# A decoder layer on one core: state-space work of the next sequence moved into the stage before, routing and W2 sums reordered

## The chip, the core and the metric

The kernel runs on one core of a Trainium2 chip. It has five engines with their own instruction queues: TensorE (PE, with weight loads listed as PEld), VectorE (DVE), ScalarE (ACT), GpSimd (POOL) and SyncE (SP, here used for DMA only). Each queue is worked off in order; semaphores make one engine wait for another. The metric is the device time of one execution in microseconds.

## The reference

Four sequences of 256 tokens with 256 channels go through three blocks, each followed by residual and layer norm:

```python
x = _layernorm(x + _L0_attn_ref(x, ...))          # retention, 16 heads, group norm, SiLU gate
x = _layernorm(x + _L0_xattn_ref(ctx_1024, x, ...))  # state-space block on ctx, gated by silu(x)
x = _layernorm(x + _L0_ffn_ref(x, ...))           # 2 of 8 LoRA experts
# state-space block: 256 channels, 16 states, 256 steps
u = silu(causal_conv4(in_proj @ ctx) + conv_b)
dt_lo, Bm, Cm = split(x_proj @ u)
delta = softplus(dt_proj @ dt_lo + dt_proj_b)
state = state * exp(delta * A) + (delta * u) * Bm ;  y = sum_n(state * Cm) + D * u ;  y = y * silu(z)
# experts: for each of the 2 chosen experts k of a token
x1 = x @ W1.T + lora1 ; x3 = x @ W3.T + lora3 ; h = silu(x1) * x3
out += (h @ W2.T + lora2(h)) * rw[k]              # rw: the two top probabilities, normalised
```

## The kernel before

The work is a pipeline over the four sequences. `batches` calls `stage(b, fb)` on every engine: stage 0 does retention and state space of sequence 0 alone; stages 1 to 3, a hardware loop (`Fori`), do retention and state space of sequence `b` together with the experts of `fb = b - 1`; the last stage does the experts of sequence 3.

A stage has a start (`first` or `later`), a loop over 14 slots `n` and a tail. The slots are `MAIN`: chunk `m` of the 896 hidden channels (7 chunks of 128) for the chosen expert `k` (0 or 1). For each slot TensorE runs `base` (W1, W3 on x2, once per chunk: 12 fp32r matmuls of 256 columns) and `hidden` (the LoRA part, 12 more); ScalarE a tanh; VectorE two products (`fs`, then `fq`, here called halves); GpSimd the product with the expert's weight `rwT` (L532) and, for k = 1, the sum `xsums[m]`; TensorE `shrink` (A2) two slots later. In the tail TensorE sums W2 over `xsums` (`down`, 7 times 4 matmuls) and adds B2 in PSUM bank `acc`; VectorE adds the residual (`r3`), normalises and SyncE stores.

The state-space scan is cut into 16 units of 128 x 512. `SCANS` says which slot does which unit. A unit is: ScalarE `decays` (two Exp), GpSimd `drive_unit` (L450, du times a row of B from DRAM), VectorE `scan` (L1246) and `times_c` (L1256), and TensorE `add_states`, four transposing matmuls that add it into `acc`. The ring of units has four places, so a drive waits for the add of the unit four before it. Two units share one pair of rows of B and C that SyncE fetches in `spread`.

Before the scans a stage needs: `context` (input projection, gen bank `IN`), `conv` on VectorE (L1196, six steps of 256 columns), tanh, `u` (L1199), `low_rank` (`DBL`), `step_size` matmuls (`DT`), ScalarE `softplus` (L613 Abs, L617 Exp, L619 Ln, L607 Relu; Ln lies in another activation table than Exp and Tanh), VectorE `step_size` (L1220 to L1228) and GpSimd `du` (L491). All of this stands in `later`, at the start of the stage.

Also in `later`: for the experts of `fb`, the transposes of x2, the router's logits, `route` on VectorE (L1462 to L1489, 24 small dependent steps, 22 of them in part 1), the flip of the routing rows (`rt`), `spread_rows`, the experts' low-rank inputs (`expert_inputs`, A1 and A3, into `a2p`), `masked_inputs` and the split of them into high and low parts `am`. Retention needs Q, K, V, GATE projections, then in slots 0 to 4 eight `scores`, `decayed` and `values`, the group norm in slots 4 to 7, the output projection at n = 9 and `r1` at n = 10 (L1411), its statistics and GpSimd root (L476), the normalised `x1` at n = 12 (L647). At the end comes the gate of the state-space block: tanh of x1 (L775), `zs` (L1417), its transposes `token_z`, `zT` (L641), `r2` (L1423, L1425), `x2` (L647).

PSUM: two `gen` banks used in turn in the order of `LATER` and `GEN_END`; `xf` banks 0 and 1 for hidden slots, bank 2 is `acc`; `a2p` two banks; `ret` for retention; `acc` for y and then for the W2 sums, which is why `down` waits until `r2` has read y:

```python
if b is not None:
    need(pe, "r2_ready", b, 2)
    for m in range(FM - 1):
        down(fb, m)
```

## Time and profile before

| | us |
|---|---|
| median of 3 runs | 509.28 |
| lowest, highest | 505.58, 509.33 |
| the profiled execution | 509.72 |
| its span, first to last instruction | 508.0 |
| TensorE busy | 407.3 (80%) |
| VectorE busy | 360.5 (71%) |
| GpSimd busy | 271.6 (53%) |
| ScalarE busy | 200.8 (40%) |

The profile is of one execution. Busy shares are sums over the span; ends of matmuls are modelled and follow one another closely, so their lengths overlap a little. In a timeline a row gives the start, the length of the group, engine, line, operation, tiles, the number of instructions, and in brackets how long the engine stood idle before it and what ended that. Nearly all matmuls have line 792, a helper, and are told apart by their tiles.

### The profile page before, as it was taken

What the parts mean: (1) busy time and instruction counts of PE and PEld (TensorE: products, weight loads), DVE (VectorE), ACT (ScalarE), POOL (GpSimd) and SP (SyncE); (2) the same over time, 40 slices, a digit from 0 to 9 for tenths busy, and PEclk for the clock granted to TensorE, in tenths of its full rate; (3) what the DMA queues carried; (4) which work ended last, traced back from release to release, by engine and by line L of the source; (5) the groups of instructions that cost most, each with busy time, mean ns of one, the idle gap of its engine ahead of it and who ended that gap; (6) DMA issues with size and microseconds to landing.
All of it is one profiled execution on the core that took longest, in us unless ns stands there. A gap on an engine that the chain in (4) does not pass through costs nothing.

```text
span 508.0 us, 7806 instructions
## 1 busy us (share of the span) xinstructions
PE 407.3 (80%) x2416; PEld 330.7 (65%) x2416; DVE 360.5 (71%) x657; ACT 200.8 (40%) x467; POOL 271.6 (53%) x245
## 2 busy tenths in 40 slices
PE   3748535598799878986999878976999868789994
PEld 2433324376679767864779767764779757679993
DVE  4347999677879997377789996488789994642224
ACT  2757244258543322358443322367442322141100
POOL 6239975334854885207745975208546973033331
PEclk9979656789899989999799989998899999959999
DMA  6592654003021220011111210030112100000000
GB/s 213 95 249 86 201 169 157 22 3 105 11 70 47 83 53 21 20 43 65 41 41 55 70 63 12 22 85 22 41 41 83 48 14 1 21 1 1 1 1 21
DMA packets 16542, 30.44 MB, mean 60 GB/s; under 512 B 2040, under 2 KB 5376, under 8 KB 16384
## 3 DMA queue, kind: packets, MB, share of 16 engines
q1 hardware_dynamic: 16224, 28.27, 18.5%
q10 hardware_dynamic: 288, 1.84, 1.0%
q14 instruction: 20, 0.16, 0.1%
q8 instruction: 10, 0.16, 0.1%
HBM read 28.66 MB, written 1.44 MB: 59 GB/s over the span
## 4 chain that ended last, share of the span: by engine, by line
PE 38%; issue 25%; DVE 23%; POOL 6%; ACT 5%; DMA 1%; DVEq 1%; SPq 0%; POOLq 0%; ACTq 0%
PE xf L792 15%; DVE ring L1246 12%; PE gen L792 9%; PE a2p L792 6%; PE acc L792 4%; PE ret L792 3%; DVE fth L1365 2%; DVE ring L1256 2%; POOL ring L450 1%; POOL rs L476 1%; DMA wattn_sb<-in_wattn 1%; ACT am L654 1%; DVE work L1370 1%; DVE gscale L1402 1%; POOL wsplit L459 1%
## 5 line engine op out<-in xcount | busy, mean ns | idle before, releaser
L450 POOL TENSOR_TENSOR ring<-cv,brow 128x512 f32<-128x512 f32 x64 | 104.4, 1640 | 27.8 <-PE acc L792 18.6
L1246 DVE TENSOR_TENSOR_SCAN ring<-decay,ring 128x512 f32<-128x512 f32 x64 | 102.6, 1603 | 2.1 <-POOL ring L450 2.1
L792 PE MATMUL xf<-am,wsplit 128*128 128x256 f32 x672 | 99.4, 299 | 5.0 <-DVE am L1326 5.0
L792 PEld LDWEIGHTS xf<-am,wsplit 128*128 128x128 f32 x672 | 89.4, 199 | 11.7 <-DVE am L1326 8.1
L532 POOL TENSOR_TENSOR work<-work,rwT 128x256 f32<-128x256 f32 x56 | 55.9, 998 | 64.8 <-DVE work L1370 64.8
L568 ACT ACTIVATE decay<-dt_w,nega 128x255 f32<-128x255 f32 x128 | 57.6, 498 | 72.9 <-DVE ring L1246 72.8
L792 PE MATMUL a2p<-work,wff_sb 128*128 128x256 f32 x288 | 75.2, 390 | 0.5 <-POOL work L532 0.5
L792 PE MATMUL acc<-ident,ring 128*128 128x128 f32 x256 | 43.6, 299 | 39.5 <-DVE ring L1256 39.2
L1256 DVE TENSOR_TENSOR ring<-ring,crow 128x512 f32<-128x512 f32 x64 | 68.3, 1067 | 3.2
L792 PEld LDWEIGHTS acc<-ident,ring 128*128 128x128 f32 x256 | 32.3, 152 | 54.4 <-DVE ring L1256 49.7
L748 ACT ACTIVATE fth<-xf 128x256 f32<-128x256 f32 x56 | 21.0, 375 | 97.2 <-PE xf L792 97.1
L792 PEld LDWEIGHTS a2p<-work,wff_sb 128*128 128x128 f32 x288 | 51.7, 193 | 10.5 <-issue 4.5
L792 PE MATMUL xf<-x2s,wsplit 128*128 128x256 f32 x336 | 53.3, 313 | 0.7 <-ACT rwT L728 0.7
L1365 DVE SCALAR_TENSOR_TENSOR fth<-fth,xf 128x256 f32<-128x256 f32 x56 | 23.2, 414 | 37.1 <-ACT fth L748 37.1
L792 PEld LDWEIGHTS xf<-x2s,wsplit 128*128 128x128 f32 x336 | 47.0, 208 | 2.9 <-ACT rwT L728 1.0
L476 POOL TENSOR_TENSOR rs<-ve,mhalf 128x2 f32<-128x2 f32 x12 | 11.8, 986 | 56.1 <-DVE ve L1284 56.1
L665 ACT ACTIVATE qm<-q_sb,headblk 128x128 f32<-128x128 f32 x96 | 30.4, 391 | 20.4 <-PE gen L792 20.4
L792 PE MATMUL gen<-qm,kT 128*128 128x512 f32 x64 | 35.9, 646 | 2.3 <-POOL qm L482 2.3
L1263 DVE TENSOR_TENSOR sc<-gen,dmask 128x512 f32<-128x512 f32 x32 | 22.0, 686 | 20.0 <-PE gen L792 19.5
L491 POOL TENSOR_TENSOR cv<-dt_w,u 128x512 f32<-128x512 f32 x4 | 5.1, 1264 | 55.0 <-DVE dt_w L1228 55.0
L792 PE MATMUL gen<-xT_sb,wattn_sb 128*128 128x256 f32 x96 | 27.5, 437 | 4.9 <-DMA wattn_sb<-in_wattn 3.1
L792 PEld LDWEIGHTS gen<-xT_sb,wattn_sb 128*128 128x128 f32 x96 | 20.6, 220 | 9.9 <-DMA wattn_sb<-in_wattn 3.8
(175 smaller groups left out, 582.7 us busy)
## 6 DMA issues: line engine op xcount, KB each, us to landing
brow<-bc_dram SPq DMA_DIRECT2D x32, 256.0 KB, 3.5
crow<-bc_dram SPq DMA_DIRECT2D x32, 256.0 KB, 3.3
work<-in_wsp SPq DMA_DIRECT2D x2, 896.0 KB, 7.6
work<-in_wsp ACTq DMA_DIRECT2D x2, 896.0 KB, 5.4
wff_sb<-in_wff SPq DMA_DIRECT2D x2, 896.0 KB, 6.4
wattn_sb<-in_wattn SPq DMA_DIRECT2D x1, 1280.0 KB, 5.9
xT_sb<-in_xT SPq DMA_DIRECT2D x4, 256.0 KB, 3.5
xn_sb<-in_x SPq DMA_DIRECT2D x4, 256.0 KB, 2.5
```

Of the source, the lines that this page charges most:

```text
L450: pool.tensor_tensor(ring[:, i % RING], du[:, j].unsqueeze(1).broadcast_to([P, UN, S]), brow[:, c % 2], ALU.mult).then_inc(sem["drive_read ...
L476: pool.tensor_tensor(dst[:], src[:], mhalf[:], ALU.pow).then_inc(sem[done], 1)
L491: pool.tensor_tensor(du[:], delta[:], u[:], ALU.mult).then_inc(sem["du_ready"], 1)
L532: pool.tensor_tensor(xs[:, n % 4], fq[:, n % 2], rwT[:, k], ALU.mult).then_inc(sem["xs_ready"], 1)
L568: act.activation(decay[:, i % 2, n, 1:], delta[:, j, 1:], ACT.Exp, scale=nega[:, j, s_:s_ + 1]).then_inc(sem["decay_ready"], 1)
L665: last = act.activation(qm[:, i % 2, h], q_sb[:, t, chunk * P:(chunk + 1) * P], ACT.Copy, scale=headblk[:, row:row + 1])
L748: act.activation(fth[:, n % 2], xf[XF_BANK[X_MAIN + n]][:, 0], ACT.Tanh, scale=0.5).then_inc(sem["th_ready"], 1)
L792: return pe.matmul(o, l, r, skip_group_check=True, **kw)
L1246: dve.tensor_tensor_scan(unit, flat(decay[:, i % 2]), unit, 0.0, ALU.mult, ALU.add).then_inc(sem["state_ready"], 1)
L1256: dve.tensor_tensor(unit, unit, crow[:, c % 2], ALU.mult).then_inc(sem["out_ready"], 1)
L1263: dve.tensor_tensor(sc[:, i % 2], gen[(G_SC + i) % 2][:].rearrange("p (h i) -> p h i", h=4), dmask[:, h0:h0 + 4], ALU.mult).then_inc(sem[" ...
L1365: dve.scalar_tensor_tensor(fs[:, n % 2], fth[:, n % 2], 1.0, o[:, 0], ALU.add, ALU.mult).then_inc(sem["s_ready"], 1)
```

## The change

- The loop over the stages is written out: no `Fori`, every wait is on a constant. The order of the gen banks is one list over all stages.
- For the next sequence `b + 1` these move from the start of its stage into stage `b`: `context` (n = 8), convolution (9), `u` and `DBL` (10), `DT` (11), softplus and step sizes (12), `du` and the first drives (12, 13), decays 0 and 1 (13); then, in the tail, scans 0 and 1 (`EARLY`), Q, decays 2 and 3, drives 2 and 3. Scans 2 to 4 (`PROLOGUE`) run in the start of the stage, 5 to 15 in slots 0 to 9.
- The transposes of x2, the logits and the routing of sequence `b` run in the tail of stage `b`, ahead of B2 on TensorE, instead of at the start of the next stage.
- The W2 sums and B2 accumulate in `ret` instead of `acc`; `down` 0 to 4 run right after the last shrink, 5 and 6 after the logits. `xf` bank 2 is `ret`.
- The expert weights: expert 0 has weight 1 and expert 1 the ratio of the two; the common factor `share` is multiplied in `r3`. So the product with k = 0 goes from VectorE straight into `xs`, without GpSimd. Routing has two steps fewer (22, 20 of them in part 1).
- `r1`, `dt_e`, `cth`, `dt_abs` live in other buffers (`qm`, `gth`). SyncE stores `b - 2` and reloads inputs between the B and C rows.

The diff, cut to its core:

```diff
 
-SCANS = [[0], [1], [2], [3, 4], [5], [6], [7], [8, 9], [10], [11, 12], [13, 14], [15], [], []]
+FIRST_SCANS = [[0], [1], [2], [3, 4], [5, 6], [7, 8], [9, 10], [11, 12], [13], [14], [15], [], [], []]
+SCANS = [[5], [6], [7], [8], [9], [10], [11, 12], [13], [14], [15], [], [], [], []]
+EARLY, PROLOGUE = [0, 1], [2, 3, 4]
+N_IN, N_CONV, N_U, N_DBL, N_DT, N_STEP = 8, 9, 10, 10, 11, 12
+
+
+def scans(b, n):
+    return (SCANS if b else FIRST_SCANS)[n] if b is not None else []
+
+
 PARTS = ((0, 0), (0, 1), (1, 0))
 POOL_MASKED = (2, 3)
 AM_ORDER = [0, 2, 1, 3]
 LAG = 2
...
 
             stage(0, None)
-            with eng.Fori(1, B) as b:
+            for b in range(1, B):
                 stage(b, b - 1)
             stage(None, B - 1)
...
                 for c in range(DS // UN):
+                    if c == 2 and b >= 2:
+                        store(b - 2)
+                    if c == 3 and b + 1 < B:
+                        reload(b + 1)
 
...
                     need(pool, "y_part", b, i - RING + 2)
+                elif b > 0:
+                    need(pool, "y_part", b, i - RING + 1)
...
+                    step_input(b)
                     drive_unit(b, 0)
                     drive_unit(b, 1)
-                    if fb is not None:
-                        for i in POOL_MASKED:
-                            masked(b, i)
+                elif b is not None:
+                    drive_unit(b, 4)
+                    drive_unit(b, 5)
+                    for i in POOL_MASKED:
+                        masked(b, i)
+                    cross_queries(b)
+                    drive_unit(b, 6)
                 if fb is not None:
 
...
                                                ).then_inc(sem["xsum_ready"], 1)
+                    if b is not None and n == 12 and b + 1 < B:
+                        step_input(b + 1)
+                        drive_unit(b + 1, 0)
                     if b is not None and n == 13:
                         root(b, ve, rs, "r2_ready", 9, "r2_pow")
+                        if b + 1 < B:
+                            drive_unit(b + 1, 1)
                         if fb is None:
                             split_low(range(3 * PER_W, BLOCKS))
+                if b is not None and b + 1 < B:
+                    drive_unit(b + 1, 2)
+                    drive_unit(b + 1, 3)
+                    residual(b + 1)
...
                 for j in range(2):
                     act.activation(dt_abs[:, j], g[:, j], ACT.Abs, bias=v_("dtb")[:, j:j + 1]).then_inc(sem["dt_parts"], 1)
-                if isinstance(b, int):
+                if b == 0:
                     positive(b, g)
                 need(act, "dt_parts", b, 2)
                 act.activation(dt_e, dt_abs[:], ACT.Exp, scale=-1.0).then_inc(sem["dt_exp"], 1)
                 need(act, "dt_exp", b, 1)
...
+            def tail(b):
+
+                need(act, "keep_ready", b, 0)
+                normed(b, r2, x2, "r2_shift", "x2_ready")
+                need(act, "xf_filled", b, X_X2 + 1)
+                need(act, "xs_ready", b, 0)
+                act.wait_ge(sem["w_low_b3"], PER_W)
+                act.activation(x2T, xf[XF_BANK[X_X2]][:], ACT.Copy).then_inc(sem["x2T_ready"], 1)
+                act.activation(x2s[:, 0], xf[XF_BANK[X_X2]][:], ACT.Copy).then_inc(sem["x2T_ready"], 1)
+                if b + 1 < B:
+                    queries(b + 1)
+                    start_y(b + 1)
+                need(act, "rt_step", b, 2)
+                act.activation(le[:], lg[:], ACT.Exp).then_inc(sem["lg_exp"], 1)
+                if b + 1 < B:
+                    for i in EARLY:
+                        decays(b + 1, i + 2)
+
             def later(b, fb):
...
-                    low_rank(b)
-                    softplus(b)
                     masked(b, 1)
...
-                    decays(b, 0)
+                    decays(b, PROLOGUE[0] + 2)
                 am_high(fb, (2, 3))
                 if b is not None:
-                    decays(b, 1)
+                    for i in PROLOGUE[1:]:
+                        decays(b, i + 2)
...
                             if i + 2 < UNITS:
                                 decays(b, i + 2)
+                        if b + 1 < B:
+                            if n == N_IN:
+                                conv_input(b + 1)
+                            if n == N_CONV:
+                                conv_tanh(b + 1)
+                            if n == N_DBL + 1:
+                                low_rank(b + 1)
+                            if n == N_STEP:
+                                softplus(b + 1)
                         if n == 7:
                             need(act, "gn_step", b, 12)
...
-                    need(act, "keep_ready", b, 0)
-                    normed(b, r2, x2, "r2_shift", "x2_ready")
+                    tail(b)
 
             batches(act, stage)
...
+
                 if b is not None:
-                    token_values(b)
-                    low_rank(b)
...
                 need(pe, "a2_ready", fb, 0)
                 expert_inputs(0, A1)
                 if b is not None:
-                    step_size(b)
+                    token_values(b)
                 expert_inputs(1, A3)
                 if b is not None:
+                    token_keys(b)
                     project(b, "GATE", wg)
+                    start_y(b)
+                    for i in EARLY:
+                        add_states(b, i)
                 base(fb, 0)
 
                 xf_free(fb, X_RT)
...
                     scores(b, 1)
+                    for i in PROLOGUE[:2]:
+                        add_states(b, i)
                 else:
                     base(fb, 1)
...
-                                start_y(b, fb)
-                            else:
-                                for i in SCANS[n - 1]:
-                                    add_states(b, i)
+                            for i in (scans(b, n - 1) if n > 0 else PROLOGUE[2:]):
+                                add_states(b, i)
                         if 1 <= n <= 4:
...
+                        if n == N_IN and b + 1 < B:
+                            context(b + 1)
+                        if n == N_DBL and b + 1 < B:
+                            low_rank(b + 1)
+                        if n == N_DT and b + 1 < B:
+                            step_size(b + 1)
...
                                 for k in range(2):
                                     last = mm(g[:, t], ro[:, k, t * P:(t + 1) * P], wo[:, k], start=(k == 0), stop=(k == 1))
                             last.then_inc(sem["gen_filled"], 1)
                 if fb is not None:
+                    shrink(fb, len(MAIN) - 1)
                     if b is not None:
-                        need(pe, "r2_ready", b, 2)
-                        for m in range(FM - 1):
+                        need(pe, "ro_lin", b, 2)
+                        for m in range(W2_FIRST):
                             down(fb, m)
-                    shrink(fb, len(MAIN) - 1)
-                    down(fb, FM - 1)
+                if b is not None:
+                    flip_x2(b)
+                    if b + 1 < B:
+                        need(pe, "x_in", b + 1, 16)
+                        project(b + 1, "Q", wq)
+                    logits(b)
+                if fb is not None:
+                    for m in range(W2_FIRST if b is not None else FM - 1, FM):
+                        down(fb, m)
                     need(pe, "a2_ready", fb, 3)
                     for t in range(NT):
                         for k in range(2):
-                            last = mm(acc[:, t], a2m[:, 0, k, t * P:(t + 1) * P], B2[:, k], start=False, stop=(k == 1))
...
-                    conv(b)
                     token_values(b)
-                need(dve, "x2T_ready", fb, 2)
-                dve.tensor_tensor(x2s[:, 1], xf[XF_BANK[X_X2]][:], x2s[:, 0], ALU.subtract).then_inc(sem["xl_ready"], 1)
-                route(fb, 0)
-                if b is not None:
                     token_keys(b)
-                route(fb, 1)
-                if b is not None:
-                    step_size(b)
+                    scan(b, PROLOGUE[0])
+                    times_c(b, PROLOGUE[0])
                     chunk_state(b)
                 need(dve, "a_filled", fb, 2)
...
                     gate_silu(b)
+                    for i in PROLOGUE[1:]:
+                        scan(b, i)
+                        times_c(b, i)
 
...
+                            need(dve, "xs_used", fb, max(n - 3, 0))
+                            need(dve, "xsum_ready", fb, MAIN[n - 4][0] + 1 if n >= 4 else 0)
+                            product = xs[:, n % 4]
+                        else:
+                            need(dve, "xs_ready", fb, max(m - 1, 0))
+                            product = fq[:, m % 2]
+                        dve.tensor_tensor(product, fs[:, n % 2], o[:, 1], ALU.mult).then_inc(sem["q3_ready"], 1)
+                    if b is not None and n == 11:
                         norm_shift(b, mv, rs, nm, "r1_pow", "r1_shift")
...
                             norm_stats(b, r1, st, mv, ve, "r1_ready", 1)
+                        if n == N_CONV and b + 1 < B:
+                            conv(b + 1)
+                        if n == N_U and b + 1 < B:
+                            gated_conv(b + 1)
...
                             dve.scalar_tensor_tensor(zs[:], zth[:], 1.0, x1[:], ALU.add, ALU.mult).then_inc(sem["r2_ready"], 1)
+                            if b + 1 < B:
+                                step_size(b + 1)
                             if fb is None:
...
+                early = EARLY if b is not None and b + 1 < B else []
+                for i in early[:1]:
+                    scan(b + 1, i)
+                if b is not None:
+                    norm_shift(b, mv, rs, nm, "r2_pow", "r2_shift")
+                for i in early[:1]:
+                    times_c(b + 1, i)
                 if fb is not None:
                     second_input(fb, 1)
                     need(dve, "a2_ready", fb, 2)
                     dve.tensor_tensor(a2m[:, 0], a2m[:, 0], a2m[:, 1], ALU.add).then_inc(sem["a2_ready"], 1)
                 if b is not None:
-                    norm_shift(b, mv, rs, nm, "r2_pow", "r2_shift")
+                    need(dve, "x2T_ready", b, 2)
+                    dve.tensor_tensor(x2s[:, 1], xf[XF_BANK[X_X2]][:], x2s[:, 0], ALU.subtract).then_inc(sem["xl_ready"], 1)
+                for i in early[1:]:
+                    scan(b + 1, i)
+                if b is not None:
+                    route(b, 0)
+                for i in early[1:]:
+                    times_c(b + 1, i)
+                if b is not None:
+                    route(b, 1)
                 if fb is not None:
                     need(dve, "down_done", fb, 1)
                     need(dve, "keep_ready", fb, 1)
-                    dve.tensor_tensor(r3[:], acc[:], keep[:], ALU.add).then_inc(sem["r3_ready"], 1)
-                    norm_stats(fb, r3, st3, mv3, ve3, "r3_ready", 1)
+                    for t in range(NT):
+                        dve.scalar_tensor_tensor(r3[:, t], ret[:, t], share[:, fb % 2, t:t + 1], keep[:, t], ALU.mult, ALU.add
+                                                 ).then_inc(sem["r3_ready"], 1)
+                    norm_stats(fb, r3, st3, mv3, ve3, "r3_ready", 2)
                     norm_apply(fb, r3, mv3, rs3, yo, "r3_pow", "y_ready")
 
```

## Rows read from the trace of the kernel before

**Rows 1.** Stretches table: stretch and length in us, busy time by engine (instructions), PEclk, DMA, GB/s
```profile
0.00:95.80 95.80, 50.33 (x223) 32.00 (x223) 67.50 (x97) 45.74 (x103) 58.96 (x65) 0.79 0.54 158
95.80:123.60 27.80, 25.80 (x108) 18.85 (x108) 19.11 (x55) 15.95 (x37) 11.65 (x11) 0.87 0.13 41
...
235.80:306.20 70.40, 62.07 (x425) 52.84 (x426) 62.75 (x86) 27.69 (x69) 49.25 (x37) 0.93 0.17 53
306.20:322.80 16.60, 14.29 (x73) 11.81 (x72) 7.84 (x20) 4.06 (x8) 5.20 (x6) 1.00 0.01 1
322.80:348.00 25.20, 21.61 (x109) 16.25 (x107) 16.76 (x56) 15.73 (x36) 7.96 (x8) 1.00 0.20 57
...
435.20:452.20 17.00, 12.37 (x64) 10.40 (x63) 10.90 (x41) 4.73 (x10) 0.69 (x1) 0.77 0.04 16
452.20:508.00 55.80, 48.70 (x321) 45.07 (x320) 16.59 (x41) 6.78 (x17) 19.87 (x25) 0.96 0.02 6
```

**Rows 2.** Instructions on tile `ring`, one stage (213.6 to 325.8): ns min/median/max
```profile
L1246 DVE TENSOR_TENSOR_SCAN ring<-decay,ring x16: 1211/1514/2286, 238.9 to 304.4; 128x512 f32<-128x512 f32 x16
...
L1256 DVE TENSOR_TENSOR ring<-ring,crow x16: 680/968/1595, 241.7 to 306.4; 128x512 f32<-128x512 f32 x16
```

**Rows 3.** Timeline of TensorE, products 8 and 12 of stage 2: start, length
```profile
280.27 1.57 PE L792 MATMUL xf<-am,wsplit 128*128 128x256 f32 x12
...
304.58 1.56 PE L792 MATMUL xf<-am,wsplit 128*128 128x256 f32 x12
```

**Rows 4.** Timeline of stage 2's end, VectorE, the last row TensorE
```profile
308.32 0.70 DVE L1417 SCALAR_TENSOR_TENSOR kT<-kT,q_sb 128x512 f32<-128x512 f32 x1 [0.47 <-ACT kT L775]
...
313.01 0.88 DVE L1425 TENSOR_TENSOR dt_w<-dt_w,q_sb 128x512 f32<-128x512 f32 x1
...
314.93 3.62 PE L792 MATMUL acc<-wff_sb,sc 128*128 128x256 f32 x16
```

**Rows 5.** Timeline at the loop's seam, VectorE, then TensorE, stage 2
```profile
216.60 2.46 DVE L1196 SCALAR_TENSOR_TENSOR cv<-xpad,cwh,cv 128x256 f32<-128x256 f32 x6 [2.35 <-issue]
...
220.59 1.05 PE L792 MATMUL gen<-u,wssm_sb 128*40 128x256 f32 x4 [2.50 <-DVE u L1199]
```

**Rows 6.** Timeline around the first product, TensorE, the last row VectorE
```profile
229.79 0.61 PE L792 MATMUL acc<-ident,rt 128*20 128x128 f32 x4
...
241.01 1.12 PE L792 MATMUL acc<-ident,yT 128*128 128x128 f32 x4 [2.79 <-ACT yT L636]
...
238.91 2.29 DVE L1246 TENSOR_TENSOR_SCAN ring<-decay,ring 128x512 f32<-128x512 f32 x1
```

**Rows 7.** Timeline of ScalarE: softplus of stage 2, normalisation ahead of z
```profile
224.83 0.84 ACT L613 ACTIVATE yT<-gen,vec_sb 128x256 f32<-128x256 f32 x2 [1.91 <-PE gen L792]
...
226.35 1.28 ACT L619 ACT_TABLE_LOAD   x1
227.64 0.63 ACT L619 ACTIVATE yT<-ring 128x512 f32<-128x512 f32 x1
...
306.54 1.08 ACT L647 ACTIVATE q_sb<-dt_w,nm,rs 128x256 f32<-128x256 f32 x2
```

**Rows 8.** Groups by line, GpSimd, the same stage
```profile
L450 POOL TENSOR_TENSOR ring<-cv,brow 128x512 f32<-128x512 f32 x16 | 25.8, 1622 | 6.4 <-PE acc L792 6.2 <-POOL cv L491 0.2
L532 POOL TENSOR_TENSOR work<-work,rwT 128x256 f32<-128x256 f32 x14 | 15.2, 1085 | 13.2 <-DVE work L1370 13.2
```

**Rows 9.** Timeline of stage 2's start, VectorE, the last row GpSimd
```profile
219.76 0.69 DVE L1199 SCALAR_TENSOR_TENSOR u<-ring,cv 128x512 f32<-128x512 f32 x1 [0.69 <-ACT ring L586]
...
222.81 0.16 DVE L1469 TENSOR_REDUCE t<-le 128x2 f32<-128x16 f32 x1
...
227.47 0.43 DVE L1220 TENSOR_SCALAR dt_w<-ring 128x512 f32<-128x512 f32 x1
...
230.25 1.26 POOL L491 TENSOR_TENSOR cv<-dt_w,u 128x512 f32<-128x512 f32 x1 [14.03 <-DVE dt_w L1228]
```

**Rows 10.** Timeline of VectorE, end of stage 0
```profile
95.71 0.69 DVE L1423 TENSOR_TENSOR dt_w<-acc,yT 128x512 f32<-128x512 f32 x1 [0.90 <-ACT yT L641]
```

308 lines of the change are left out of this document (152 added, 156 removed).

## The prediction

> **What bounds the kernel now.** I read the stretches table first. One loop stage takes 112.2 us and I cut it at three marks. H is the first expert product (`hidden(fb, 0)`), X the end of `hidden(fb, 12)`, T the end of the B2 product. H to X takes 70.4, X to T 16.6, T to the next H 25.2. The whole span is then 123.6 to the first H, twice 112.2, 104.2 for stage 3 (348.0 to 452.2), and 55.8 for the last: 508.0 [rows 1]. In none of them is one engine at full load, so each has its own last wait.
>
> In H to X the last part is VectorE's. It carries the 16 scan units of the stage, each a scan of 1.51 and a product with C of 0.97 in the median [rows 2]. From the start of product 8 to that of product 12 TensorE takes 24.3 us [rows 3]. Its own work there (four products, two bases, four shrinks, eight to nine adds, one output projection) comes to about 17 at 0.23 us for an fp32 matmul of 256 columns (3.62 for 16, [rows 4]) and 1.4 to 1.5 for twelve fp32r ones. So 7 us are waits for VectorE.
>
> From T to H the chain runs through the seam of the loop: VectorE starts the convolution after 2.35 us that are put down to issue, works 2.5 on it, and TensorE waits 2.5 for `u` [rows 5]. The routing flip comes at 229.79 [rows 6] and H 6.0 later. From X to T the chain is normalise, tanh, `zs`, transpose, `zT`, `r2`, and then TensorE's W2 sums [rows 4, 7].
>
> **The change part by part.** Nothing large disappears. Seven of 14 GpSimd products per stage (1.09 each, [rows 8]) and two routing instructions go; the rest moves to another place. What counts is therefore which waits open and close.
>
> *T to H.* Context, Q, flip, logits, DBL and DT leave this stretch. TensorE has left K, A1, V, A3 and GATE (40 matmuls, 9.0), key transpose and `y` start (1.0), the adds of units 0 and 1 (0.9) and base 0 (1.5): 12.4, then from the routing flip to H the 6.0 of before, since the ScalarE/VectorE chain between them stays. That is 18.4 against 25.2, a gain of 6.8. The routing does not hold it up: 22 instructions of part 1 take 4.66 (222.81 to 227.47, [rows 9]), the new one has 20, and I find it ending 2 us after T, while its reader comes 12 us after T.
>
> At H something new is last. TensorE now has `add_states(3)` before `hidden(fb, 0)`, and it needs `times_c(3)`. VectorE does unit 3 only after `gate_silu`: the scan would begin where that of unit 0 begins now, 238.91, and takes 2.29 there [rows 6], its product 0.7 to 1.0 [rows 2]. So H's matmuls start 6 us later than the mark. Before, TensorE stood until 241.01 in any case, for `yT` [rows 6]; the net loss is 2 (bounds 0 and 6), and I book it in H to X.
>
> *H to X, stages 1 and 2.* VectorE does 13 units instead of 16 after H, gains the convolution (2.46) and `u` (0.69) [rows 5, 9]. That is 7.4 less, 3.2 more. It lets TensorE run product 8 to 12 at its own pace: 17.5 with the three moved small projections, plus a new wait. `low_rank(b+1)` stands in TensorE's queue at n=10 behind nothing else, and its `u` comes on VectorE after product 10's two halves, `r1`, its statistics: 2.9 us idle. 20.7 against 24.3, a gain of 3.6. With the 2 from above H to X becomes 68.8.
>
> *X to T, stages 1 and 2.* ScalarE at n=12 now runs tanh 12, then `softplus(b+1)`, and only then the normalisation and tanh of the z chain. Softplus is Abs, Exp, a table load, Ln, Relu: 224.83 to 228.27 plus 0.8 for the two Relu, 4.2. The tanh then needs its table back, 1.28 more [rows 7]. The z tanh ends 7.6 after X, `zs` 8.3 (now it starts at 308.32, 2.1 after X, [rows 4]), and TensorE, which is through at X+4.2, waits 4. VectorE goes on with `step_size`, 2.7 (227.47 until GpSimd starts at 230.25, [rows 9]), then halves 13 and `r2`: ready at X+13.0 against 7.7 now [rows 4]. GpSimd's last xs product sits behind `step_input` and `drive_unit(b+1, 0)` (1.26, [rows 9], and 1.62, [rows 8]) that wait for the same step size, so the shrink 13 comes at X+14.9. From there TensorE has shrink, seven W2 sums, flip, Q, logits, B2: 4+28+8+8 matmuls at 0.23 plus 1.3, 12.1. T = X+27.0; the price is 10.4, bounds 7 (chains overlap better) and 14. I add 0.5 for VectorE's token values, which now follow `r3`.
>
> The period is 68.8 + 27.0 + 18.9 = 114.7, 2.5 more than 112.2; low 109, high 119.
>
> *Stage 0.* It gets all moved work and gives none up: convolution 2.5 and unit 15 now ahead of `r1` (1.9 at the shortest times of [rows 2]), then the serial chain `u`, DBL, `dbl`, DT, softplus, table load (0.7+1.1+0.4+1.1+4.2+1.3 = 8.8), `step_size` between `zs` and `r2` (1.7 net), scan 0 of the next sequence ahead of the shift (1.2). Now `r2` starts at 95.71 [rows 10]; I expect 110. The first H moves from 123.6 to 139.7: +16. Bounds: +8, if most of the chain lies beside other work, and +19.
>
> *Stage 3.* No next sequence: no softplus in the tail. H to X loses 2.7 of projections and the 2.9 wait, 63.2. X to T: flip and logits inside, the gaps filled, 17.3. T to H: A1, A3, base 0, then 7.2 as now from the routing flip, 12.5 against 17.0. 93.0 against 104.2, a gain of 11.2 (bounds 9 and 15). The last stage stays 55.8.
>
> *Sum.* 139.7 + 2 x 114.7 + 93.0 + 55.8 = 517.9. The profiled execution lies 1.7 above its span (509.72 against 508.0), so 519.6; it is 0.4 above the median of 509.28. I say 519.
>
> *Loads and buffers.* The new SyncE order puts `store(b-2)` ahead of the B rows for unit 4 and `reload` ahead of those for unit 6. I price them at nothing: the store waits for `y_ready` at about T+6, and unit 4's drive is needed only near H, some 12 us later. If that cover went, its drive (1.62, [rows 8]) and the load ahead of it would come on top of H, bounded by the 6 us that H stands anyway.
>
> **Two rules against the rows.** Softplus has its table load at 226.35, 1.28 long, and the next activation starts at 227.64 [rows 7]. The Trainium skill, page "ScalarE: Activation LUTs", section "What ACT_TABLE_LOAD costs", puts a switch at 2.66 us, with a drain of 1.38 behind the load. The trace shows no such gap; by the page two switches in three tails would make the sum 8 us larger, 528.
> The loop's seam shows 2.35 of issue on VectorE [rows 5]. The Trainium skill, "Runtime: NRT & Kernel Launch", section "Instruction fetch mechanics", says that a taken branch can break the sequential prefetch and prefers unrolled code. The row agrees; but as VectorE is not last from T to H any more, it is inside the 6.8. If it came on top, the sum would be 515.
>
> **The rivals.**
> *Faster, the two engines stop hindering each other.* A unit costs VectorE 2.48, but the shortest scan took 1.21 and the shortest product 0.68 [rows 2]: 0.59 a unit, 38 us over 64 units. GpSimd sheds 7 x 1.09 a stage. If 22 of the 38 came back where VectorE is last (stage 0 and H to X), H to X would come to the 62 us that TensorE is busy [rows 1] and stage 0 would pay 8 instead of 16: 519 - 2 x 6.8 - 8 = 497. It decides from 15 us on (below 504), some 40% of the 38. For it: VectorE is last in stage 0. Against: `drive_unit` (16 x 1.62, [rows 8]) stays as it is, and work squeezed into less time overlaps more. 0.25.
> *No change, the costs of stage 0 are half hidden.* +8, and a period of 112 as before: 131.6 + 224 + 93 + 55.8 + 1.7 = 506; with +12, 510. Here the softplus chain would lie beside VectorE's last scans. 0.20.
> *Slower still, TensorE's clock.* TensorE stands 4 and then 6 us in the new tail and 6 at H. In 435.2 to 452.2, where it has such waits, the granted clock averages 0.77 of 2.4 GHz, in the three parts of the loop stage 0.93 to 1.00 [rows 1]. If 12 us of tail ran at 1.2 GHz for a half, and H as well, 5 to 6 a stage: 534. 0.13.
> *Forecast*, the moved chain in front of z costs what the seam gives and stage 0 pays once: 513 to 527. 0.42.
>
> **How the numbers follow.** About 1% is what a measurement of this kernel can tell from no change: 504 to 514.4. Slower: 0.42 + 0.13 less a little, 0.54; same 0.20; faster 0.26. The likeliest gives 519, its own range 513 to 527. For 8 in 10 the range must take in part of the faster rival and of the slow one: 498 to 532.
>
> **What would show it.** In the changed profile: ScalarE's Ln load between tanh 12 and the z normalisation; TensorE idle before `token_z` (about 4) and before shrink 13 (about 6); a wait on `times_c(3)` ahead of the first product; the first product at 140 and not near 124; T to H at 18 to 19; stage 3 at 93. Wrong it would be if scan units fell to 2.0 us, if the period were below 110, or if `u` and the step sizes came early enough that `r2` stands no later than 8 after X.

## The result: slower by 5.6%

The changed kernel took 536.67 us (median of 4 runs, 536.15 to 538.09), the kernel before 509.17 beside it; the ratio is 1.0562, 95% interval [1.0511, 1.0613]. The forecast was 519 with a range of 498 to 532. The direction was right; the size was 18 us too small, and the time lies outside the range.

The profiled execution of the changed kernel has a span of 535.3 (before: 508.0). Cut at the same marks H, X and T as before, its stretches table reads as follows (columns as in [rows 1]). H is here only a mark: the routing flip plus 6.0 us (139.49 plus 6.0 for the first), where the first product would start if nothing new stood ahead of it. In the last stage it is the product's own start.

```profile
0.00:145.50 145.50, 77.22 (x345) 51.90 (x345) 97.32 (x156) 68.34 (x154) 77.94 (x78) 0.77 0.41 120
145.50:220.20 74.70, 62.79 (x424) 52.88 (x425) 59.73 (x89) 24.34 (x62) 35.80 (x30) 0.91 0.14 42
220.20:249.20 29.00, 19.02 (x90) 16.18 (x89) 17.38 (x38) 15.46 (x31) 11.94 (x9) 0.82 0.07 23
249.20:266.90 17.70, 16.93 (x92) 13.50 (x91) 10.69 (x34) 7.69 (x20) 5.36 (x5) 1.00 0.35 81
266.90:340.90 74.00, 62.07 (x425) 52.00 (x426) 59.28 (x89) 24.34 (x62) 35.85 (x30) 0.93 0.14 41
340.90:369.30 28.40, 18.88 (x91) 16.04 (x89) 17.41 (x38) 15.46 (x31) 11.95 (x9) 0.82 0.09 28
369.30:387.00 17.70, 16.90 (x92) 13.49 (x90) 10.69 (x34) 7.71 (x21) 5.40 (x5) 1.00 0.18 59
387.00:452.30 65.30, 56.86 (x412) 49.01 (x413) 56.32 (x82) 22.05 (x57) 35.55 (x30) 0.95 0.11 37
452.30:468.90 16.60, 14.98 (x83) 13.08 (x82) 10.27 (x33) 5.37 (x11) 2.15 (x3) 1.00 0.00 0
468.90:478.50 9.60, 8.15 (x50) 6.90 (x49) 6.27 (x22) 3.05 (x6) 0.69 (x1) 1.00 0.08 29
478.50:535.30 56.80, 47.95 (x322) 44.10 (x320) 18.14 (x44) 7.01 (x17) 14.73 (x18) 0.98 0.02 5
```

| part | before | forecast | measured | forecast missed by |
|---|---|---|---|---|
| start to the first H mark | 123.6 | 139.7 | 145.5 | +5.8 |
| stage 1: H to X, X to T, T to H | 70.4, 16.6, 25.2 | 68.8, 27.0, 18.9 | 74.7, 29.0, 17.7 | +6.7 |
| stage 2 | the same | the same | 74.0, 28.4, 17.7 | +5.4 |
| stage 3 | 104.2 | 93.0 | 91.5 | -1.5 |
| last stage | 55.8 | 55.8 | 56.8 | +1.0 |
| span | 508.0 | 517.9 | 535.3 | +17.4 |

Two stretches of the stage stand out. X to T holds 19 us of TensorE work in 29 us, at a granted clock of 0.82; before, it held 14.3 in 16.6 at 1.00 [rows 1]. And H to X, which was to become shorter, is 4 us longer with the same 62 us of TensorE work. TensorE's timeline (start, length, what it did, idle time before it and what ended it) shows where it stands. The row at 152.57 is ahead of the first product, the one at 211.15 ahead of product 11 of stage 1, those from 228.64 on are the tail.

```profile
152.57 1.12 PE L856 MATMUL acc<-ident,ring 128*128 128x128 f32 x4 [7.85 <-DVE ring L1336]
153.33 2.91 PE L856 MATMUL xf<-am,wsplit 128*128 128x256 f32 x12
...
211.15 1.03 PE L856 MATMUL gen<-u,wssm_sb 128*40 128x256 f32 x4 [3.74 <-DVE u L1279]
212.11 2.48 PE L856 MATMUL xf<-am,wsplit 128*128 128x256 f32 x12
...
228.64 0.63 PE L1071 MATMUL gen<-ident,kT 128*128 128x128 f32 x4 [4.27 <-DVE kT L1503]
234.98 2.07 PE L856 MATMUL a2p<-work,wff_sb 128*128 128x256 f32 x4 [5.71 <-POOL work L574]
236.84 3.44 PE L856 MATMUL ret<-wff_sb,xsum 128*128 128x256 f32 x8
```

These are the four waits that the forecast named: unit 3's product, `u`, `token_z`, the last shrink product. It had them at 6, 2.9, about 4 and about 6 us. Behind the first, the second and the last, the same instructions take longer than elsewhere: twelve matmuls of a product 2.91 and 2.48 us instead of the 1.57 of [rows 3], eight W2 matmuls 3.44 instead of 1.9. That is not new at H. The kernel before has it there too, behind its own wait for `yT` (2.79, [rows 6]):

```profile
241.78 2.91 PE L792 MATMUL xf<-x2s,wsplit 128*128 128x256 f32 x12
244.48 2.49 PE L792 MATMUL xf<-am,wsplit 128*128 128x256 f32 x12
```

From H to product 8 TensorE is busy 41.2 of 44.5 us before and 41.4 of 49.6 (stage 1) and 40.7 of 48.9 (stage 2) in the changed kernel, at granted clocks of 0.92, 0.90 and 0.93. So what this part lost is waiting, about 4.9 us a stage, and not slower matmuls.

The chain that leads to the third and fourth wait, on ScalarE, VectorE and GpSimd:

```profile
222.20 1.28 ACT L669 ACT_TABLE_LOAD   x1
223.35 1.02 PE L856 MATMUL a2p<-work,wff_sb 128*128 128x256 f32 x4
223.49 0.63 ACT L669 ACTIVATE gth<-qm 128x512 f32<-128x512 f32 x1
224.03 0.82 ACT L655 ACTIVATE ring<-gen,vec_sb 128x256 f32<-128x256 f32 x2
224.74 1.08 ACT L698 ACTIVATE q_sb<-qm,nm,rs 128x256 f32<-128x256 f32 x2
225.84 1.28 ACT L837 ACT_TABLE_LOAD   x1
227.14 0.63 ACT L837 ACTIVATE kT<-q_sb 128x512 f32<-128x512 f32 x1
...
227.80 0.69 DVE L1503 SCALAR_TENSOR_TENSOR kT<-kT,q_sb 128x512 f32<-128x512 f32 x1 [6.10 <-ACT kT L837]
...
231.08 1.27 POOL L523 TENSOR_TENSOR cv<-dt_w,u 128x512 f32<-128x512 f32 x1 [13.56 <-DVE dt_w L1308]
...
231.71 0.68 DVE L1511 TENSOR_TENSOR qm<-acc,yT 128x512 f32<-128x512 f32 x1
...
234.20 0.72 POOL L574 TENSOR_TENSOR work<-work,ratioT 128x256 f32<-128x256 f32 x1
```

Softplus with its table load stands ahead of z on ScalarE, so `zs` comes 7.6 after X (2.1 before, [rows 4]); the step size stands ahead of `r2` on VectorE; `step_input` and drive 0 stand ahead of the last ratio product on GpSimd. One order was not tried: softplus ahead of tanh 12. The `DT` bank is full at 217.3, and ScalarE stands idle for 5.13 us until tanh 12 starts at 220.41.

### The profile page after: what moved, and what is told of

It reads as the page before. It is cut to its first block and busy times, and to the rows that moved or that the text cites. A ratio compares the mean times of both kernels' runs of the same rounds, so it can differ in the third digit from the quotient of the medians.

```text
span 535.3 us, 6819 instructions
## 1 busy us (share of the span) xinstructions
PE 401.8 (75%) x2412; PEld 329.1 (61%) x2412; DVE 363.5 (68%) x653; ACT 200.8 (38%) x467; POOL 237.4 (44%) x215
## 3 DMA queue, kind: packets, MB, share of 16 engines
q1 hardware_dynamic: 16224, 28.27, 18.1%
## 5 line engine op out<-in xcount | busy, mean ns | idle before, releaser
L478 POOL TENSOR_TENSOR ring<-cv,brow 128x512 f32<-128x512 f32 x64 | 97.7, 1534 | 69.1 <-PE acc L856 44.4
L1326 DVE TENSOR_TENSOR_SCAN ring<-decay,ring 128x512 f32<-128x512 f32 x64 | 101.4, 1585 | 2.1 <-POOL ring L478 2.1
L856 PE MATMUL acc<-ident,ring 128*128 128x128 f32 x256 | 45.6, 310 | 51.7 <-DVE ring L1336 51.7
L856 PEld LDWEIGHTS acc<-ident,ring 128*128 128x128 f32 x256 | 33.9, 157 | 65.8 <-DVE ring L1336 59.7
L1336 DVE TENSOR_TENSOR ring<-ring,crow 128x512 f32<-128x512 f32 x64 | 66.5, 1040 | 3.0
L574 POOL TENSOR_TENSOR work<-work,ratioT 128x256 f32<-128x256 f32 x28 | 23.1, 825 | 94.8 <-DVE work L1454 92.2
L856 PE MATMUL xf<-x2s,wsplit 128*128 128x256 f32 x336 | 49.1, 295 | 0.5 <-ACT ratioT L782 0.5
L856 PEld LDWEIGHTS xf<-x2s,wsplit 128*128 128x128 f32 x336 | 43.0, 191 | 3.2 <-issue 1.4
L856 PE MATMUL gen<-xT_sb,wattn_sb 128*128 128x256 f32 x96 | 25.9, 418 | 6.0 <-DVE vpad L1287 3.1
L1343 DVE TENSOR_TENSOR sc<-gen,dmask 128x512 f32<-128x512 f32 x32 | 21.9, 684 | 9.4 <-PE gen L856 9.1
L856 PEld LDWEIGHTS gen<-xT_sb,wattn_sb 128*128 128x128 f32 x96 | 19.3, 210 | 10.1 <-DMA wattn_sb<-in_wattn 3.6
```

What stands on the lines that cost most here:

```text
L478: pool.tensor_tensor(ring[:, i % RING], du[:, j].unsqueeze(1).broadcast_to([P, UN, S]), brow[:, c % 2], ALU.mult).then_inc(sem["drive_read ...
L574: pool.tensor_tensor(xs[:, n % 4], fq[:, m % 2], ratioT[:], ALU.mult).then_inc(sem["xs_ready"], 1)
L856: return pe.matmul(o, l, r, skip_group_check=True, **kw)
L1326: dve.tensor_tensor_scan(unit, flat(decay[:, i % 2]), unit, 0.0, ALU.mult, ALU.add).then_inc(sem["state_ready"], 1)
L1336: dve.tensor_tensor(unit, unit, crow[:, c % 2], ALU.mult).then_inc(sem["out_ready"], 1)
L1343: dve.tensor_tensor(sc[:, i % 2], g[:].rearrange("p (h i) -> p h i", h=4), dmask[:, h0:h0 + 4], ALU.mult).then_inc(sem["sc_ready"], 1)
```

## The experiments

All numbers are in us. The kernels down to scans_behind start from the changed kernel, those from before_unrolled on from the kernel before; each ratio is to runs of the kernel before on the same chip, so ratios compare better than medians. "First flip" is the start of the first routing flip; a stage is the distance to the next one (stages 1, 2 and 3), "rest" what follows the last flip; these columns are of one profiled execution each. unrolled_relief leaves out expert 0's weight and so computes something else; it shows time only.

| kernel | time | ratio to before, 95% interval | first flip | stages 1, 2, 3 | rest |
|---|---|---|---|---|---|
| before | 509.17 | 1 | 118.3 | 111.5, 112.3, 102.9 | 63.1 |
| changed | 536.67 | 1.0562 [1.0511, 1.0613] | 139.5 | 121.4, 120.1, 92.8 | 61.5 |
| z_first | 531.0 | 1.0432 [1.0387, 1.0476] | 135.4 | 118.5, 119.0, 93.7 | 61.5 |
| dbl_later | 529.72 | 1.0394 [1.0358, 1.043] | 140.4 | 118.0, 116.7, 92.8 | 61.4 |
| add3_later | 543.0 | 1.0649 [1.0608, 1.069] | 139.0 | 122.6, 122.8, 95.5 | 61.5 |
| all_three | 526.04 | 1.0321 [1.0283, 1.036] | 136.1 | 115.1, 116.9, 95.2 | 61.4 |
| unit3_early | 530.86 | 1.0429 [1.0384, 1.0474] | 140.2 | 118.6, 119.0, 90.5 | 61.4 |
| filled_waits | 559.74 | 1.1018 [1.0975, 1.106] | 138.4 | 124.1, 124.8, 108.1 | 61.5 |
| sized_work | 533.09 | 1.0483 [1.044, 1.0527] | 137.6 | 118.3, 118.5, 93.4 | 61.5 |
| reordered | 509.41 | 0.9993 [0.9975, 1.0012] | 136.0 | 109.3, 108.4, 92.1 | 61.5 |
| order_two | 509.61 | 0.9997 [0.9972, 1.0022] | 137.1 | 109.3, 109.2, 91.6 | 61.5 |
| scans_behind | 508.27 | 0.9972 [0.9956, 0.9988] | 136.3 | 106.9, 108.9, 93.1 | 61.4 |
| before_unrolled | 505.77 | 0.9924 [0.9892, 0.9957] | 117.5 | 111.6, 110.5, 100.4 | 62.1 |
| unrolled_relief | 498.84 | 0.9799 [0.977, 0.9829] | 118.7 | 109.0, 108.7, 98.6 | 62.2 |
| only_ratio | 500.21 | 0.9755 [0.9704, 0.9805] | 118.0 | 109.5, 109.3, 100.4 | 61.9 |
| ratio_w2 | 494.07 | 0.9705 [0.9663, 0.9747] | 118.2 | 106.8, 106.5, 98.7 | 61.4 |
| not_moved | 512.57 | 1.0037 [1.0007, 1.0067] | 126.4 | 112.6, 112.6, 96.2 | 61.4 |
| flip_early | 511.36 | 1.0021 [0.9981, 1.0061] | 123.3 | 109.7, 112.6, 102.1 | 62.2 |

### z_first: softplus and step size behind the z chain

```diff
 # ScalarE
-                            if n == N_STEP:
-                                softplus(b + 1)
 ...
                             z_columns(b)
-                                decays(b + 1, 0)
-                                decays(b + 1, 1)
+                                softplus(b + 1)
 # VectorE: step_size(b + 1) and scan 0 behind norm_shift, second_input(fb, 1) and the a2 sum
 # ScalarE: decays 0, 1 behind normed(x2);  GpSimd: step_input, drive 0 behind root(r2)
```

> The changed kernel, with one thing moved: ScalarE's softplus of the next sequence stands behind z_columns instead of ahead of the z normalisation, and what hangs on it (step sizes on VectorE, step_input and drives 0 and 1 on GpSimd, decays 0 and 1) stands behind r2 and its statistics. Theory A (the serial chain softplus, table load, z is what makes the tails long; X to T is 29.0 and 28.4 in stages 1 and 2, and stage 0 ends 22 us later than before): X to T falls to about 19, the first product comes some 9 us earlier than 145.5, three tails give 27 to 30 together: about 508. Theory B (the tail is long because VectorE and GpSimd simply have more to do there, the same work in whatever order): the work stays in the tail, X to T stays at 26 or more, total above 528.

It took 531.0: the time of theory B, but not its mechanism. X to T fell as theory A has it, in stage 1 from 29.0 to 21.3, and x2's flip comes 12 us sooner in stage 0 (108.97 instead of 121.12). Yet the routing flip of stage 0 comes only 4.1 sooner, and T to the next routing flip grew from 11.7 to 17.1 in stage 1. The saved time is taken back there, where TensorE now waits for the value bank that VectorE has to read, and runs the next eight matmuls in 2.96 instead of 1.89:

```profile
247.49 2.96 PE L855 MATMUL gen<-xT_sb,wattn_sb 128*128 128x256 f32 x8 [3.47 <-DVE vpad L1286]
```

VectorE had scan 0 and its product (2.21 and 1.50, beside GpSimd's drives), scan 1, the routing and the last norm ahead of `vpad`. So the order in the tail was a cause, but what it gave was for the most part spent at the next place where TensorE waits for VectorE.

### dbl_later: the u matmuls one slot later

```diff
-N_IN, N_CONV, N_U, N_DBL, N_DT, N_STEP = 8, 9, 10, 10, 11, 12
+N_IN, N_CONV, N_U, N_DBL, N_DT, N_STEP = 8, 9, 10, 11, 12, 12
```

> The changed kernel, with DBL and DT on TensorE one slot later (n = 11 and 12). Theory A (TensorE's 3.74 us ahead of DBL wait for u in vain, and the slower clock behind it costs another 2 to 3): both go, 5 to 6 us in stages 1 and 2; the softplus that is ahead of z starts about 2 later, so 3 to 4 of them stay as gain: about 530. In stage 0, where u comes right after the adds, a loss of 1 to 2. Theory B (the chain to z is last in any case): no gain, 536 to 541.

529.72, as theory A has it: 1.7% of the kernel before for one number. The wait for `u` went from 3.74 to 1.45, and the twelve matmuls of the next product behind it take 1.57 instead of 2.48.

### add3_later: unit 3's add behind the first product

```diff
-                    for i in PROLOGUE[:2]:
+                    for i in PROLOGUE[:1]:
                         add_states(b, i)
 ...
-                            for i in (scans(b, n - 1) if n > 0 else PROLOGUE[2:]):
+                            for i in (scans(b, n - 1) if n > 0 else PROLOGUE[1:]):
```

> The changed kernel, with add_states(3) on TensorE moved from ahead of the first product to behind it. Theory A (TensorE's 7.85 us in front of it are a wait in the wrong place of the queue): the first product starts 6 to 7 us earlier, hidden 2 ends 3 to 5 earlier, at full clock; over stages 1 to 3 that is 9 to 14 us: 523 to 528. Theory B (VectorE sets the pace there, since units 3, 4 and 5 stand ahead of the first halves, whatever TensorE does): TensorE waits at the next bank instead, total within 3 us of 536.7.

543.0, slower by 6 and so outside both theories. The first product did run early, and TensorE then stood at the same result:

```profile
144.41 0.97 PE L856 MATMUL xf<-am,wsplit 128*128 128x256 f32 x6 [0.23 <-DVE am L1401]
145.86 0.97 PE L856 MATMUL xf<-am,wsplit 128*128 128x256 f32 x6 [0.49 <-DVE am L1401]
152.05 1.11 PE L856 MATMUL acc<-ident,ring 128*128 128x128 f32 x4 [5.21 <-DVE ring L1336]
155.86 1.12 PE L856 MATMUL acc<-ident,ring 128*128 128x128 f32 x4 [2.70 <-DVE ring L1336]
156.63 2.91 PE L856 MATMUL xf<-x2s,wsplit 128*128 128x256 f32 x12
159.34 2.57 PE L856 MATMUL xf<-am,wsplit 128*128 128x256 f32 x12
```

5.21 + 2.70 is about the old 7.85. Moving the waiter does nothing when the thing waited for does not come sooner. The stages are 1.2, 2.7 and 2.7 longer. Part of that is in the rows: the base matmuls and product 1 take 2.91 and 2.57 here, in the changed kernel 2.08 and 1.58, and product 1 ends 1.8 us later behind the routing flip. For the rest I have no row.

### all_three: the three edits together

> All three moves together. If each wait is a place in a queue and they add up: 536.7 - 28 - 12 - 8 = 489, faster than the kernel before by 4%. If they hide one another (one wait removed is taken over by the next): 500 to 510. If the moved work itself is what costs, above 515.

526.04, 10.6 below the changed kernel and 17 above the one before; that is 2.4% of before, while the first two alone gave 1.3 and 1.7 (and the third cost 0.9). So the three edits nearly add up (2.1 against 2.4), and the kernel still stands above the 515 that the expectation gave to the moved work itself. The named waits are real, and they are not the whole.

### unit3_early: scan 3 into VectorE's gap

VectorE stands idle for 4.18 at 137, until the KV bank is there. Scan 3 and its product have all their inputs by then.

```diff
-                    scan(b, PROLOGUE[0])
-                    times_c(b, PROLOGUE[0])
+                    for i in PROLOGUE[:2]:
+                        scan(b, i)
+                        times_c(b, i)
                     chunk_state(b)
```

> The changed kernel with scan 3 and its product moved ahead of chunk_state on VectorE, into the 4.18 us in which VectorE stands idle there waiting for the KV bank; scans 4 onward stay. Theory A (order): the 7.85 us that TensorE waits for the product of unit 3 ahead of the first expert product is an accident of VectorE's order, so the wait goes under 1 us, the first product comes 6 us sooner behind the routing flip in stages 1 to 3, the clock dip after it vanishes too, and the kernel takes about 519 us. Theory B (the wait only moves): masked inputs, low parts and scan 4 are as late as before, so TensorE waits at hidden(0) or at unit 4 instead, a stage keeps its length within 1 us and the kernel takes 534 us or more.

530.86, between the two theories: the wait of 7.85 is gone, a wait of 5.21 for unit 4 stands behind the first product in its place, and 2.8, 1.1 and 2.3 a stage are left over as gain. Scan 3 takes 1.22 in the gap, where GpSimd is idle, and took 2.28 at its old place. Where the waited-for work was moved (here) it helped, where the waiter was moved (add3_later) it did not.

### reordered: all of it, and VectorE's tail

z_first, dbl_later and unit3_early, and beyond them:

```diff
 # VectorE's tail: low part of x2, routing, then scans 0 and 1
-                for i in early[:1]:
-                    scan(b + 1, i)
-                    times_c(b + 1, i)
 ...
                 if b is not None:
                     route(b, 0)
+                for i in early[:1]:
+                    scan(b + 1, i)
 ...
 # the last norm of the sequence before behind the next token values and keys
                     token_values(b)
                     token_keys(b)
+                finish(fb - 1)
```

> The changed kernel with softplus behind z_columns (as in z_first), N_DBL, N_DT = 11, 12 (as in dbl_later), scan 3 ahead of chunk_state, and VectorE's tail in the order low part of x2, route, scan 0, scan 1; the residual norm of the sequence before goes behind the next token values and keys, so that GATE's bank comes free earlier. Theory A: the waits add up and each of them stands on the path, so from 526.0 us (three of the edits together) it falls by a further 6 us at scan 3 and 3 us in the tail for each of three stages, to about 500 us, under the kernel before. Theory B: the path has other work right behind each wait (VectorE's whole load of a stage, the clock), and the kernel stays at 515 us or more.

509.41: as fast as the kernel before, 27.3 below the changed one, with the same instructions (TensorE 402.0 us busy, VectorE 362.9, ScalarE 199.9; in the changed kernel 401.8, 363.5 and 200.8). So the loss of the changed kernel against the one before can be undone by order alone. It came out between the 500 of theory A and the 515 of theory B.

### order_two and scans_behind: further in the same direction

```diff
 # order_two
+ TensorE: unit 4 added behind hidden(1)
+ ScalarE: decays 0, 1 behind the two copies of the turned x2; decay 3 behind the keys
 # scans_behind, on top of it
+ VectorE: scans 4 and 5 behind score masks 0, 1 and the first expert product
```

> The kernel of the run reordered with three waits more taken out: TensorE adds unit 4 behind hidden(1) instead of behind hidden(0) (wait of 4.8 to 5.2 us three times), ScalarE makes decays 0 and 1 behind the two copies of the turned x2 instead of ahead of them (TensorE's logits wait 2.1 us), and decay 3 behind the keys (TensorE's keys product waits 7.6 us for kT in the first turn). Theory A: what is left of the change's loss is such waits, so about 4 us a stage and 6 in the first come off 509.4 us: 492 to 497 us, faster than the kernel before. Theory B: VectorE's or TensorE's own work bounds the stage by now (TensorE stands still only where it has nothing that could run): 505 us or more.

> The kernel of the run order_two, with scans 4 and 5 behind the first two score masks and the first expert product on VectorE (and decay 6 behind the first tanh on ScalarE). In order_two VectorE is busy 9.90 of 10 us ahead of the first score mask, with scan 4, its product and scan 5 at 2.3, 1.5 and 2.3 us beside GpSimd's drives, and TensorE waits 5.0 us for that mask, while the first expert product, ready at 254.7, is taken up at 263.4. Theory A (order within VectorE's list): the masks come 6 us sooner, the wait of 4 to 5 us goes, and three stages give 4 us each: about 497 us. Theory B (VectorE's load): scans 4 and 5 are only late elsewhere, the ring is free later and TensorE waits for sums instead: 506 to 512 us.

509.61 and 508.27, both theory B. In order_two the waits that were taken out come back under another name, in the table of TensorE's waits (total, times, longest):

```profile
PE gen L855 <- DVE vpad L1288: 15.2, 4, 7.4
PE ret L855 <- DVE sc L1344: 15.2, 3, 5.2
```

Between 252 and 262 VectorE is busy for 9.90 of 10 us there and TensorE for 4.83. In scans_behind the wait for `sc` is gone, and the waits for scan results are back at 42.2 in all (order_two: 25.2). In these two steps order gave nothing more; that VectorE's load around H is the limit is what the rows suggest, and no run takes load off VectorE in this kernel to show it.

### filled_waits and sized_work: is it the clock?

Idle products into the free retention bank keep TensorE at work in the tail's two waits; the waits and their causes stay.

```diff
+            def idle_work(b, count):
+                need(pe, "ro_lin", b, 2)
+                for k in range(count):
+                    mm(ret[:, k % 2], ident[:], wq[:, k % 2], start=(k == 0), stop=(k == count - 1))
 # filled_waits: 16 ahead of token_z, 22 ahead of the last shrink; sized_work: 9 and 12, stages 1 and 2 only
```

> The changed kernel with idle work on TensorE in its two waits at the end of stages 1 to 3: 16 products of 128x128 by 128x256 float32 into the free retention bank ahead of token_z, and 22 ahead of the last shrink product (W2's first sum clears the bank again). Waits and their causes stay, only TensorE is not idle in them. Theory A (clock): the slower granted clock behind the waits is a loss of its own: shrink 13 takes 1.0 instead of 2.07 us and the first 8 W2 sums 1.9 instead of 3.44, 2.5 us a stage come off in stages 1 and 2, some in 3: 529 to 532 us. Theory B: the waits alone carry the loss: 535 to 539 us.

> As filled_waits, but sized to the waits: 9 idle products ahead of token_z and 12 ahead of the last shrink product, in stages 1 and 2 only (a product took 0.22 us there, so 2 us in a wait of 4.3 and 2.6 in one of 5.7; in filled_waits 16 and 22 of them overran the waits, above all in stage 3, whose waits are short). Theory A (clock): shrink 13 takes 1.0 instead of 2.07 and the first 8 W2 sums 1.9 instead of 3.44 us, so 2.6 us a stage come off: about 531 us. Theory B: nothing: 535 us or more.

filled_waits told little about the time: 22 idle products took 9.66 us in a wait of 5.7, and in stage 3, which has no such waits, they came on top (stage 3: 108.1 instead of 92.8). But its rows behind the waits were at once short. sized_work took 533.09, between its two theories: 0.8% of the kernel before, or 4 us, less than the changed kernel, and the intervals of the two ratios just overlap. So the size rests on the rows. An idle product shows as two matmuls; nine took 4.05 us and twelve 5.35, nearly the whole of the waits and not half, as the expectation has it:

```profile
225.92 0.63 PE L1071 MATMUL gen<-ident,kT 128*128 128x128 f32 x4 [0.39 <-DVE kT L1513]
226.39 5.35 PE L856 MATMUL ret<-wattn_sb,ident 128*128 128x256 f32 x24
232.26 1.13 PE L856 MATMUL a2p<-work,wff_sb 128*128 128x256 f32 x4 [0.53 <-POOL work L574]
233.23 1.89 PE L856 MATMUL ret<-wff_sb,xsum 128*128 128x256 f32 x8
```

The last shrink takes 1.13 instead of 2.07 and the W2 matmuls 1.89 instead of 3.44; the shrink still starts where it did, 14.8 behind X. The granted clock from `token_z` to x2's flip reads 1.00, in the changed kernel 0.64, and X to T is 26.6 instead of 29.0 in stage 1. So the granted clock behind the tail's waits is a loss of its own of about 2 us a stage. The larger part of the 12 us that X to T grew is waits: TensorE is idle 10.0 us in it, before 2.3. What is left is moved work.

### before_unrolled: the loops alone

```diff
-            with eng.Fori(1, B) as b:
+            for b in range(1, B):
                 stage(b, b - 1)
```

> The kernel before with its two loops (all engines' loop over sequences 1 to 3, SyncE's over 1 and 2) written out by Python, nothing else. Theory A: the seam between iterations (2.35 and 2.50 us of issue on VectorE and TensorE ahead of the first conv step and the u matmuls) stands on the path, so 2 or 3 seams give 4 to 7 us: 502 to 505 us. Theory B: it is hidden or comes back as instruction loading: 508 to 510 us.

505.77, 0.8% faster, close to theory A. (The 2.50 that the expectation calls issue on TensorE is its wait for `u` in [rows 5].) VectorE starts the convolution with no gap (before: 2.35 put down to issue, [rows 5]):

```profile
214.44 3.94 DVE L1196 SCALAR_TENSOR_TENSOR cv<-xpad,cwh,cv 128x256 f32<-128x256 f32 x6
```

### unrolled_relief and only_ratio: GpSimd's products

unrolled_relief leaves out expert 0's weight; only_ratio makes the same saving and keeps the result, as the changed kernel does, by the ratio and a common share.

```diff
-                        pool.tensor_tensor(xs[:, n % 4], fq[:, n % 2], rwT[:, k], ALU.mult).then_inc(sem["xs_ready"], 1)
+                        if k == 1:
+                            pool.tensor_tensor(xs[:, n % 4], fq[:, m % 2], rwT[:, k], ALU.mult).then_inc(sem["xs_ready"], 1)
 # only_ratio: ratioT for rwT[:, k]; route with 22 steps; r3 = acc * share + keep
```

> The unrolled kernel before, with the product of expert 0 left out on GpSimd (VectorE writes its masked product straight into xs, so the weight of the first expert is left out of the result; 7 of 14 GpSimd products of 128x256 a stage fall away). Theory A: TensorE's expert products bound this stretch and GpSimd's relief is worth nothing: within 1.5 us of the unrolled kernel. Theory B: fewer GpSimd products let VectorE's scans and products run nearer to 1.21 and 0.69 us, and the shrink products wait less: 4 us or more below the unrolled kernel.

> The unrolled kernel before with the ratio's way of routing of the changed kernel (expert 1 weighted by its ratio to expert 0, the common share applied in the last residual; route with 22 steps instead of 24 and NR 18 instead of 20): the whole of what is asked of GpSimd's relief in unrolled_relief, but with nothing left out. Theory A (GpSimd's 7 products a stage hinder): as fast as unrolled_relief, 498 to 500 us, 9 to 11 us under the kernel before. Theory B (unrolled_relief gained from something else, such as the early store into xs without the weight's wait): 503 us or more.

498.84 and 500.21: some 6 us below before_unrolled, theory B of the first and theory A of the second. From product 8 to 12 of stage 2, where TensorE waits only for scan results, these waits fell from 5.4 to 3.6 us and the stretch from 24.5 to 22.8. The scans:

```profile
L1246 DVE TENSOR_TENSOR_SCAN ring<-decay,ring x64: 1194/1508/2292, 25.4 to 411.9; 128x512 f32<-128x512 f32 x64
```

```profile
L1249 DVE TENSOR_TENSOR_SCAN ring<-decay,ring x64: 1208/1272/2340, 25.3 to 407.0; 128x512 f32<-128x512 f32 x64
```

(the first row is of before_unrolled, the second of unrolled_relief; ns min/median/max). The median overstates it: it jumps from the slow scans to the fast ones. The mean of a scan fell only from 1611 to 1558 ns, 3.4 us over all 64, and VectorE's whole busy time from 364.7 to 359.3.

The mechanism of the rival in which the two engines stop hindering each other is there, and this saving is worth 1.3% on its own. How much of the 1.3% comes of it is open: expert 0's products also reach TensorE without the step on GpSimd, and no run parts the two, since only_ratio does both as well.

### ratio_w2: the W2 sums in retention's bank

```diff
-        xf.append(acc)
+        xf.append(ret)
-                    mm(acc[:, t], xsums[m][:, t * P:(t + 1) * P], W2[:, m], start=(m == 0 and t == 0), stop=False)
+                    mm(ret[:, t], xsums[m][:, t * P:(t + 1) * P], W2[:, m], start=(m == 0 and t == 0), stop=False)
-                        need(pe, "r2_ready", b, 2)
+                        need(pe, "ro_lin", b, 2)
```

> The kernel of the run only_ratio with the W2 and B2 sums in retention's bank (they no longer wait for r2, and the routing flip and mask differences use that bank too), while x2's flip and the routing stay in the head of the next stage. Theory A (the bank is not what makes not_moved 12 us slower than only_ratio, the early routing ahead of the next convolution on VectorE is): as only_ratio or up to 4 us below it, since the wait of 1.5 us a stage for r2 goes: 496 to 501 us. Theory B (the bank costs): 504 us or more.

494.07, ratio 0.9705: the fastest kernel of the study, faster than both. The medians are 6 us below only_ratio; the two ratios, 0.9755 and 0.9705, have intervals that overlap, so how much this step gives is not settled. In the rows, TensorE no longer waits for `r2` ahead of the sums (1.48 a stage in only_ratio), and a stage fell from 109.4 to 106.7.

### not_moved and flip_early: x2's flip ahead of the last sums

```diff
 # not_moved, on ratio_w2: TensorE's order at the end of a stage
+                    for m in range(5):
+                        down(fb, m)
+                if b is not None:
+                    flip_x2(b)
+                    logits(b)
+                    for m in range(5 if b is not None else FM - 1, FM):
+                        down(fb, m)
 # and: ScalarE's copies and exponential, VectorE's low part and routing in the tail
 # flip_early: the exponential, the low part and the routing back behind the convolution
```

> The change without its main part: loops written out, the ratio's way of routing, W2 and B2 sums in retention's bank, x2's flip, logits and routing ahead of the last two W2 sums and B2, but convolution, step sizes and first scans of the next sequence stay at the head of its own stage. Theory A (the move of this work is the whole loss): 490 to 500 us, so the move costs the changed kernel 37 to 47 us. Theory B (W2 in retention's bank or the earlier flip, which makes TensorE, ScalarE and VectorE stand in line for the end of the z chain, costs too): 504 us or more.

> The kernel of the run not_moved with the low part of x2 and the routing on VectorE, and the exponential on ScalarE, back in the head of the next stage behind the convolution; x2's flip and its logits on TensorE and the two copies on ScalarE stay ahead of the last W2 sums and B2. Theory A (VectorE's order is what costs not_moved 18.5 us against ratio_w2: routing and the last norm stand ahead of the convolution, u comes late, wait of 4.3 instead of 1.7 us): 494 to 499 us. Theory B (TensorE and ScalarE standing for the flip's chain costs): most of it stays, 505 us or more.

512.57 and 511.36, theory B of both. They are 17 to 19 us slower than ratio_w2 (3.3 and 3.2% by the ratios), and they hardly differ from each other: it is not VectorE's order of the routing, it is where TensorE does the flip and the logits and ScalarE the two copies. In the following rows of ratio_w2 and then flip_early, `kT` through `ident` is token_z, `ctx_sb` the next context, `u` the matmuls on the gated convolution.

```profile
196.61 0.60 PE L1013 MATMUL gen<-ident,kT 128*128 128x128 f32 x4
...
206.60 1.03 PE L793 MATMUL gen<-ctx_sb,wssm_sb 128*128 128x256 f32 x4
207.46 1.89 PE L793 MATMUL gen<-xT_sb,wattn_sb 128*128 128x256 f32 x8
209.19 0.60 PE L1051 MATMUL xf<-ident,x 128*128 128x128 f32 x4
...
215.88 1.03 PE L793 MATMUL gen<-u,wssm_sb 128*40 128x256 f32 x4 [1.74 <-DVE u L1210]
```

```profile
201.43 0.60 PE L1012 MATMUL gen<-ident,kT 128*128 128x128 f32 x4
202.92 1.13 PE L792 MATMUL a2p<-work,wff_sb 128*128 128x256 f32 x4 [0.89 <-POOL work L533]
...
208.70 0.63 PE L1045 MATMUL xf<-ident,x 128*128 128x128 f32 x4 [0.33 <-ACT x L648]
210.06 1.03 PE L792 MATMUL xf<-wroute_sb,work 128*128 128x8 f32 x8 [0.73 <-issue]
...
214.48 1.03 PE L792 MATMUL gen<-ctx_sb,wssm_sb 128*128 128x256 f32 x4
...
223.77 1.03 PE L792 MATMUL gen<-u,wssm_sb 128*40 128x256 f32 x4 [2.94 <-ACT kT L598]
```

From the context to `u` both take 9.3, though ratio_w2 has the flip and the logits in there: the convolution's chain sets that length, and they lie in its shade. Ahead of the context they cost their own 1.6 and the waits: 13.05 from token_z to the context instead of 9.99. In stage 0 it costs 5.0, where TensorE stands 6.48 for the normed x2. Of the 18.1 between the two spans (491.7 and 509.8) stage 0 has 5.0, the stages 1 to 3 have 2.9, 6.0 and 3.4; for the second half of stage 2's 6.0 I have no row.

## Why the prediction went wrong

**Where the 17.4 us were missed.** By the table above: H to X 11.1 over stages 1 and 2, stage 0 5.8, X to T 3.4, the last stage 1.0; T to H (-2.4) and stage 3 (-1.5) went the other way.

**What bounds the kernel.** That the waits between products 8 and 12 are for VectorE's scans is right, but not their size. In the kernel before TensorE is busy 19.25 of these 24.3 us and waits 5.1 for scan results; I had added up some 17 of work from the shortest lengths and called the other 7 waits.

**T to H.** Forecast 18.9, measured 17.7: 11.7 to the routing flip, where I had 12.4 and 0.5 more. The 6.0 behind it is my mark; where nothing stands ahead of the first product (add3_later), it starts 5.5 behind the flip. The table's T to H is the part where the change gives what it says, 7.5 a stage.

**The wait at H.** Named rightly, mis-sized. I put unit 3's scan at 2.29 and its product at 0.7 to 1.0; they took 2.28 and 1.57, the product too beside GpSimd's drives. TensorE stood for 7.85 and went on 7.1 behind the mark, not 6. The first product, 2.91 instead of 1.57, and the add of unit 4 now stand behind this wait, and the base matmuls behind them are 0.8 shorter than before (2.08 for 2.91). Product 1 starts 4.9 and 4.2 us later than before in stages 1 and 2, where I had booked 2.

**H to X.** I booked a gain of 3.6 from product 8 to 12 (24.3 to 20.7); it was 0.6 (23.7). TensorE's own work there was put at 17.5 and is 19.95; the `u` wait was 3.74 instead of 2.9 (and 17.5 + 2.9 is 20.4, not 20.7). Of these 2.4 more, 1.7 are the product and the shrink behind the new wait, at 2.48 and 1.86 instead of 1.57 and 1.03. This, with the line above, is the step that failed: the 68.8 for H to X, measured 74.7 and 74.0. It has a net of 2 for the wait on unit 3 that was 4 to 5, and a gain of 3.6 that was 0.6, because TensorE's work was added up at its shortest lengths, where the rows of the kernel before already have longer ones, and a new wait brings more of them.

**X to T.** `zs` was put at X+8.3 and came at X+7.6, `r2` was to be ready at X+13.0 and was at X+12.9, the last shrink X+14.9 and X+14.8. The chain was right to a microsecond. What followed it was put at 12.1 and took 14.2: the first matmuls behind a wait. The rows of sized_work show the same matmuls short once the wait is filled.

**Stage 0.** `r2` forecast at 110, came at 114.06, and TensorE then stood 10.4 for the normed x2. All of the serial chain lies open there; the upper bound of +19 was still too low against the measured +21.9.

**Stage 3.** 91.5 against 93.0, but in part by luck: H to X took 65.3 for 63.2, X to T 16.6 for 17.3, and T to H 9.6 for 12.5, so the misses cancel.

**The two rules.** The load of the Ln table starts at 222.20 and takes 1.28, and the next activation starts at 223.49: no drain of the size that the Trainium skill gives ("ScalarE: Activation LUTs", "What ACT_TABLE_LOAD costs") is to be seen, and leaving it out of the sum was right. On the loop's seam the Trainium skill ("Runtime: NRT & Kernel Launch", "Instruction fetch mechanics") prefers unrolled code, and the runs agree: 0.8% for the loops alone, and the gap of 2.35 is gone. I had counted it inside the 6.8. That instruction fetch is what filled the gap no run shows.

**The rivals.** The clock rival said 534 and had 0.13. Its time was nearest, and the clock is part of the answer, but a small one: about 2 us a stage in the tail (sized_work) and 1.7 behind `u`, and at H nothing against the kernel before, where the rival had 5 to 6 for tail and H together. That it named the time best is mostly luck; the larger part were the sizes of the waits. Of the rival of the two engines the mechanism is there (unrolled_relief) and the size wrong: 1.3% for the whole saving, and not 4. One of my signs of being wrong even came true: by the medians of a stage a unit fell from 2.48 to 1.93 us (scan 1.24, product 0.69). The means say 2.62 and 2.55, so the median was the wrong thing to watch.

**Where the 27 us lie.** By whole steps: loops written out 505.8, the ratio 500.2, W2 in retention's bank 494.1, flip and routing ahead of the last sums 512.6, and the moved convolution, step sizes and scans 536.7. So three parts gain some 15 us, of which the forecast had credited only the loops, and two lose some 43: the flip and routing 18.5 by the medians and 17 by the ratios, which I had taken for free, and the moved work 24 by the medians and 27 by the ratios. The last step also changes the order of the banks, some buffers and SyncE's order, which no run takes apart. It does not lose by more work: TensorE is busy 401.8 us in the changed kernel and 402.0 in reordered, where order alone gets the loss back (509.4). Why that version does not reach the 494 of ratio_w2 is open. VectorE is full around H (order_two) and the flip stays ahead of the sums, but the moved work with the flip left in the next stage was not run.

## What to carry to other kernels

Work that is moved ahead of a chain is not paid once but with every engine's queue that it enters: ask, for ScalarE, VectorE and GpSimd in turn, which result of the present stage now stands behind it. A wait on TensorE costs its length and the slow matmuls behind it, here some 1.3 to 2.5 us at each of the three places (my estimate from the rows above); but look first whether the kernel before has such a wait in the same stretch, as it had at H, since then they are in its time already. Work that lies in the shade of another engine's chain is free where it is; before moving it, look for what the chain leaves bare, and test such a change part by part, since gains can be hidden under losses: here 15 us of gain under 43 of loss.

## What the runs showed of the hardware that I had not expected

- TensorE, behind waits of 2.8 (before) and of 3.7 to 7.9 us (changed), took 2.48 to 2.91 for twelve matmuls that take 1.57 elsewhere, and 3.44 for eight that take 1.89. In the changed tail the granted clock reads 0.82 of 2.4 GHz. With idle products in its waits the last shrink takes 1.13 instead of 2.07, the eight W2 matmuls 1.89, and the clock there reads 1.00.
- VectorE's product of 128x512 float32 takes 0.68 alone and up to 1.77 beside GpSimd; a scan 1.19 and up to 2.33 (changed kernel). Taking away 7 of GpSimd's products a stage brought the mean scan from 1611 to 1558 ns (the median from 1508 to 1272) and made the kernel 1.3% faster.
- At the loop's seam VectorE stood 2.35 us before its first instruction with nothing to wait for; written out, the gap is gone (before_unrolled).
